# Causal attention on one core: another written order of all steps, eight slots for the exponentials in place of six

## The reference, cut to what matters

```python
x = L0_attn_x                               # (4, 2048, 256)
xn = _layernorm(x)
s = attention(xn)                           # 16 heads of 16, causal
g = silu(two_local_attention_layers(xn))    # 8 heads of 64, window 128, and a gated MLP
return x + s * g

# attention, for every batch row and head
scores = q @ k.T * scale                    # scale = 16 ** -0.5
scores = where(k_pos > q_pos, -inf, scores)
p = softmax(scores)                         # over k
out = p @ v
```

## Time and profile before

| what | value |
|---|---|
| median of 3 runs | 4990.12 us (4989.68 to 5007.07) |
| profiled execution | 4986.53 us, span 4984.7 us |
| TensorE (PE) busy | 4590.0 us, 92% |
| VectorE busy | 3673.8 us, 74% |
| ScalarE busy | 2994.0 us, 60% |
| GpSimd busy | 1342.6 us, 27% |
| mean granted TensorE clock | 0.949 |

### The profile page before, as it was taken

One profiled execution on the slowest core, in us unless ns is written; L12 is line 12 of the kernel. 1 busy time (PEld: TensorE's weight loads), 2 busy tenths in 40 slices (PEclk: granted clock), 3 DMA queues, 4 the chain that ended last, 5 costly groups with the idle time before them and its releaser, 6 DMA issues. The chain is left out here.

```text
span 4984.7 us, 91933 instructions
## 1 busy us (share of the span) xinstructions
PE 4590.0 (92%) x32224; PEld 3005.9 (60%) x32224; DVE 3673.8 (74%) x7585; ACT 2994.0 (60%) x6873; POOL 1342.6 (27%) x1844
## 2 busy tenths in 40 slices
PE   8589999999999996899999999995999999999986
PEld 7433334333334332577777777764677777777766
DVE  7488887887878883777777777754777777777746
ACT  3157776777777774456565666651665656566642
POOL 3112111121111121433333333311433333333300
PEclk9789998999999997899999999996999999999998
DMA  8722432222432222000000000001000000000008
GB/s 300 212 34 35 57 45 36 36 35 41 55 42 36 36 36 69 5 9 18 10 18 10 14 13 14 14 9 65 5 18 10 18 10 18 10 14 14 14 6 277
DMA packets 174917, 214.21 MB, mean 43 GB/s; under 512 B 75068, under 2 KB 126228, under 8 KB 168340
## 3 DMA queue, kind: packets, MB, share of 16 engines
q1 hardware_dynamic: 174484, 208.56, 18.4%
HBM read 124.05 MB, written 83.89 MB: 42 GB/s over the span
## 5 line engine op out<-in xcount | busy, mean ns | idle before, releaser
L601 ACT ACTIVATE a_pt<-a_ring 128x512 f32<-128x512 f32 (+3 forms) x2560 | 1182.8, 542 | 474.4 <-PE a_ring L712 458.8
L652 DVE TENSOR_REDUCE a_mx<-a_ring 128x2 f32<-128x1024 f32 (+3 forms) x1092 | 1129.6, 1064 | 267.9 <-PE a_ring L732 164.3
L996 POOL TENSOR_TENSOR l_rn<-l_ssm,l_half 128x8 f32<-128x8 f32 x256 | 431.7, 1687 | 941.0 <-DVE l_ssm L1278 941.0
L725 PE MATMUL a_ring<-a_ks,a_qs 48*128 48x512 f32 (+3 forms) x2560 | 568.3, 439 | 115.7 <-DMA a_v_in<-v_d 83.1
L712 PE MATMUL a_ring<-a_qs,a_ks 49*128 49x512 f32 (+3 forms) x2560 | 574.3, 456 | 50.8 <-ACT a_pt L601 26.9
L749 PE MATMUL a_ot<-a_pt,a_vt 128*32 128x512 f32 (+3 forms) x5120 | 613.0, 559 | 1.8 <-ACT a_os L607 1.3
L712 PEld LDWEIGHTS a_ring<-a_qs,a_ks 49*128 49x128 f32 x2560 | 255.1, 193 | 454.9 <-ACT a_pt L601 271.8
L1097 ACT ACTIVATE l_pr<-l_pr,l_negm 128x256 f32<-128x256 f32 (+1 forms) x1024 | 501.8, 495 | 6.5 <-DVE l_negm L1330 6.1
L725 PEld LDWEIGHTS a_ring<-a_ks,a_qs 48*128 48x128 f32 x2560 | 265.9, 196 | 380.4 <-ACT a_pt L601 175.7
L575 POOL TENSOR_TENSOR a_gate<-a_gate 128x1 f32<-128x1 f32 x512 | 99.6, 195 | 1413.6 <-ACT a_pt L601 1403.4
L1003 POOL TENSOR_TENSOR l_work<-l_work,l_rot 128x512 f32<-128x512 f32 x256 | 357.4, 1397 | 396.0 <-DVE l_work L1286 396.0
(11 more groups left out here) (173 smaller groups left out, 9070.4 us busy)
## 6 DMA issues: line engine op xcount, KB each, us to landing
qk_d<-p_parts SPq DMA_DIRECT2D x16, 2048.0 KB, 10.4
a_qs<-qk_d SPq DMA_DIRECT2D x96, 256.0 KB, 8.5
a_ks<-qk_d SPq DMA_DIRECT2D x96, 256.0 KB, 18.5
x_d<-l_dx SPq DMA_DIRECT2D x32, 512.0 KB, 2.8
l_xt<-x_d SPq DMA_DIRECT2D x24, 513.0 KB, 3.8
p_x_in<-x SPq DMA_DIRECT2D x16, 512.0 KB, 8.8
x_d<-p_xt SPq DMA_DIRECT2D x16, 512.0 KB, 5.1
v_d<-p_vt SPq DMA_DIRECT2D x16, 512.0 KB, 10.8
```

Source lines behind the costliest of these rows:

```text
L601: act.activation(pt[:, (g * STEPS + s) % NPT, 2 * piece + f, q0:CHUNK], bank("step", g, k, f)[:, q0:CHUNK], ACT.Exp).then_inc(exp_done.sem, 1)
L652: r = dve.tensor_reduce(mx[:, pr, :, t, kc], ring[:, banks[0]:banks[1] + 1, 0:w], AX.X, ALU.max)
L725: mm = pe.matmul(bank("unit", G, n, f)[:, 0:w], qs[rows, v, pr, q0:q0 + P], ks[rows, v, pr, kc * CHUNK:kc * CHUNK + w], start=True, stop=k ...
L996: pool.tensor_tensor(out=rn[:, a * HEADS:(a + 1) * HEADS], in0=ssm[:, a * HEADS:(a + 1) * HEADS], in1=half[:, 0:HEADS], op=ALU.pow).then_i ...
```

## The change

NPT, the number of slots for exponentials, goes from 6 to 8. All 208 entries of TensorE's order are written anew, and the places of the rarer entries on the other queues follow. The set of entries for a group is the same. The units run two less ahead of the steps (45 to 124 in place of 47 to 126). The distance between a step and the weighing of its slot changes from place to place. On SyncE, out 1 and row_out 4 change places. No function that computes is changed.

```diff
-        NPT = 6
+        NPT = 8
...
         def tensor_order(do):
-            do("step", 0); do("unit", 47); do("weigh", -4); do("step", 1); do("unit", 48); do("step", 2)
-            do("unit", 49); do("weigh", -3); do("step", 3); do("unit", 50); do("step", 4); do("step", 5)
-            do("weigh", -2); do("weigh", -1); do("step", 6); do("step", 7); do("unit", 51); do("unit", 52)
-            do("step", 8); do("unit", 53); do("weigh", 0); do("step", 9); do("unit", 54); do("weigh", 1)
-            do("step", 10); do("unit", 55); do("step", 11); do("unit", 56); do("weigh", 2); do("row_out", 2)
-            do("unit", 57); do("step", 12); do("step", 13); do("out", -1); do("unit", 58); do("weigh", 3)
...
-            do("unit", 71); do("step", 25); do("unit", 72); do("weigh", 10); do("weigh", 11); do("unit", 73)
-            do("step", 26); do("unit", 74); do("weigh", 12); do("step", 27); do("unit", 75); do("step", 28)
-            do("unit", 76); do("step", 29); do("unit", 77); do("step", 30); do("unit", 78); do("weigh", 13)
-            do("unit", 79); do("step", 31); do("step", 32); do("weigh", 14); do("unit", 80); do("unit", 81)
-            do("step", 33); do("unit", 82); do("row_out", 3); do("step", 34); do("unit", 83); do("step", 35)
-            do("step", 36); do("weigh", 15); do("unit", 84); do("unit", 85); do("step", 37); do("unit", 86)
...
-            do("step", 48); do("weigh", 19); do("step", 49); do("unit", 96); do("step", 50); do("unit", 97)
-            do("weigh", 20); do("step", 51); do("unit", 98); do("step", 52); do("weigh", 21); do("unit", 99)
...
-            do("step", 75); do("weigh", 34); do("unit", 125); do("step", 76); do("step", 77); do("weigh", 35)
-            do("step", 78); do("step", 79); do("unit", 126); do("row_out", 5)
+            do("step", 0); do("unit", 45); do("step", 1); do("weigh", -4); do("unit", 46); do("step", 2)
+            do("unit", 47); do("weigh", -3); do("step", 3); do("weigh", -2); do("step", 4); do("step", 5)
+            do("unit", 48); do("weigh", -1); do("step", 6); do("unit", 49); do("step", 7); do("unit", 50)
+            do("weigh", 0); do("unit", 51); do("step", 8); do("unit", 52); do("step", 9); do("unit", 53)
+            do("weigh", 1); do("step", 10); do("unit", 54); do("weigh", 2); do("step", 11); do("unit", 55)
+            do("step", 12); do("row_out", 2); do("unit", 56); do("step", 13); do("out", -1); do("weigh", 3)
...
+            do("step", 28); do("weigh", 12); do("unit", 76); do("step", 29); do("step", 30); do("weigh", 13)
+            do("unit", 77); do("step", 31); do("unit", 78); do("weigh", 14); do("step", 32); do("unit", 79)
+            do("weigh", 15); do("unit", 80); do("step", 33); do("unit", 81); do("step", 34); do("unit", 82)
+            do("row_out", 3); do("out", 1); do("step", 35); do("unit", 83); do("step", 36); do("weigh", 16)
...
+            do("step", 46); do("unit", 90); do("step", 47); do("unit", 91); do("weigh", 20); do("step", 48)
+            do("unit", 92); do("step", 49); do("unit", 93); do("step", 50); do("unit", 94); do("step", 51)
+            do("unit", 95); do("weigh", 21); do("step", 52); do("unit", 96); do("unit", 97); do("step", 53)
...
+            do("step", 75); do("weigh", 34); do("step", 76); do("unit", 123); do("step", 77); do("unit", 124)
+            do("weigh", 35); do("step", 78); do("step", 79); do("row_out", 5)
...
-                do("row_out", 4); do("out", 1); do("out", 2)
+                do("out", 1); do("row_out", 4); do("out", 2)
...
-                for n in range(1, 8):
+                for n in range(1, 7):
                     do("step", n)
                 do("raw_out", -1)
-                for n in range(8, 12):
+                for n in range(7, 13):
                     do("step", n)
-                do("row_copy", 2); do("step", 12); do("step", 13); do("raw_out", 0)
+                do("row_copy", 2); do("step", 13); do("raw_out", 0)
...
-                do("row_copy", 4)
-                for n in range(45, 54):
-                    do("step", n)
-                do("raw_out", 2)
-                for n in range(54, 80):
+                do("raw_out", 2); do("step", 56); do("step", 57); do("step", 58); do("row_copy", 4)
+                for n in range(59, 80):
                     do("step", n)
```

More of the change, by code:

```diff
@@ L450, in tensor_order @@
[L450 to L454, removed]
@@ new lines, in tensor_order @@
+            do("step", 14); do("unit", 57); do("unit", 58); do("weigh", 4); do("step", 15); do("unit", 59)
+            do("step", 16); do("unit", 60); do("step", 17); do("unit", 61); do("weigh", 5); do("unit", 62)
+            do("step", 18); do("unit", 63); do("unit", 64); do("step", 19); do("out", 0); do("step", 20)
+            do("weigh", 6); do("step", 21); do("unit", 65); do("step", 22); do("unit", 66); do("weigh", 7)
+            do("unit", 67); do("unit", 68); do("step", 23); do("unit", 69); do("weigh", 8); do("step", 24)
@@ new lines, in tensor_order @@
+            do("unit", 92); do("step", 49); do("unit", 93); do("step", 50); do("unit", 94); do("step", 51)
+            do("unit", 95); do("weigh", 21); do("step", 52); do("unit", 96); do("unit", 97); do("step", 53)
+            do("weigh", 22); do("step", 54); do("unit", 98); do("step", 55); do("unit", 99); do("weigh", 23)
+            do("step", 56); do("unit", 100); do("unit", 101); do("weigh", 24); do("step", 57); do("unit", 102)
+            do("unit", 103); do("step", 58); do("weigh", 25); do("row_out", 4); do("step", 59); do("unit", 104)
@@ new lines, in tensor_order @@
+            do("step", 60); do("unit", 105); do("weigh", 26); do("unit", 106); do("step", 61); do("unit", 107)
+            do("step", 62); do("unit", 108); do("weigh", 27); do("step", 63); do("unit", 109); do("unit", 110)
+            do("step", 64); do("weigh", 28); do("step", 65); do("unit", 111); do("unit", 112); do("weigh", 29)
+            do("step", 66); do("unit", 113); do("step", 67); do("unit", 114); do("out", 2); do("step", 68)
+            do("unit", 115); do("weigh", 30); do("step", 69); do("unit", 116); do("step", 70); do("unit", 117)
@@ L461, in attend @@
+            do("weigh", 31); do("unit", 118); do("step", 71); do("unit", 119); do("step", 72); do("unit", 120)
+            do("weigh", 32); do("step", 73); do("unit", 121); do("weigh", 33); do("step", 74); do("unit", 122)
+            do("step", 75); do("weigh", 34); do("step", 76); do("unit", 123); do("step", 77); do("unit", 124)
+            do("weigh", 35); do("step", 78); do("step", 79); do("row_out", 5)
         held = [None] * NB
@@ L677, in around @@
             def around(do):
-                for n in range(0, 7):
-                    do("unit", n)
-                do("out", -3)
-                for n in range(7, 27):
+                do("unit", 0); do("unit", 1); do("unit", 2); do("out", -3)
+                for n in range(3, 35):
                     do("unit", n)
                 do("out", -2)
-                for n in range(27, 58):
+                for n in range(35, 57):
                     do("unit", n)
                 do("out", -1)
-                for n in range(58, 67):
+                for n in range(57, 65):
                     do("unit", n)
                 do("out", 0)
-                for n in range(67, 80):
+                for n in range(65, 80):
                     do("unit", n)
```

21 lines of the change are left out of this document (8 added, 13 removed).

## The result

The changed kernel is slower: 5046.51 us (median of 4 runs, 5043.51 to 5062.55) against 4994.23 us for the kernel before in the same comparison; ratio 1.0116, 95% interval [1.0088, 1.0144]. The ratio was estimated together with its interval from the runs of the comparison; the quotient of the two medians is 1.0105, inside the interval. The forecast was 4976 us and "same"; the range ended at 5022. The slower rival, a clock that falls between weighings 20 and 21, was named and had a chance of 0.20. It is what happened, at a higher price than I gave it.

The account below looks back on a forecast made before the run. TensorE was the busiest engine, losing clock mid-period in the attention stage. 15 x (-0.6 - 0.1) = -11 us, say -11 to -15, took 4986.5 to 4974; the runs' median, 3.6 above, gave 4977; forecast 4976 us, range 4930 to 5022.

Parts of the forecast that it names:

- slower rival: Between weighings 20 and 21 the clock falls where nothing covers it: 5016 us, 5025 with weigh 0 waiting; chance 0.20.
- 1. Trigger of the load: Next group's q, k, v load, queued behind row_out 2, starts 1.5 us later; bounds +1.1 and +1.9.
- 2. Work ahead of the wait: Before unit 80: two more units and one weighing; TensorE 1.7 us later, load wait from 2.6 to about 2.1 us.
- 3. Less work behind it: From unit 80 to the next group: two fewer units, one fewer weighing; -2.1 us a period.
- item 5(b): Stretch without a weighing moves to steps 48 to 51, units 92 to 95: 1.6 us in half the groups, +0.8.
- Item 5(a): Behind the load: a shorter wait keeps full clock in six groups, say, instead of three of 14; -0.5 us on average.
- Item 5(c): Two groups with lasting low clock, 13 us over the mean together: half regained as fall and wait separate, -0.4 a period.
- 6. Weighing and slots: Weighing positions and two more slots for exponentials: priced at 0, from -1.0 to +0.6 us a period.
- 7. Order inside: Sequence of entries within a group, alike in both orders: 0, plus or minus 1.0 us a period.
- 8. and 9. Queue and ends: Sync queue swap of row_out 4 and out 1: 0. Prologue -2.4 us, last group +1.7 to +2.4: together 0.

Follow-up runs that it names:

- b_slots8: The kernel before with eight slots for exponentials in place of six, order unchanged: ratio 0.9994 to the kernel before.
- a_twice_at_62: The changed kernel with the score matmuls of steps 62 to 64 done twice: ratio 1.0125 to the kernel before.
- a_spread: The changed kernel with weigh 21 behind unit 93 and weigh 22 behind unit 96, nothing added: ratio 1.0024 to the kernel before.
- b_load_late: The kernel before with row_out 2 and row_copy 2 one step later, behind step 12: ratio 1.0042 to the kernel before.
- a_load_at_11: The changed kernel with row_out 2 and row_copy 2 one step earlier, behind step 11: ratio 1.0053 to the kernel before.

## Why the prediction was wrong, point by point

1. Trigger of the load: right in kind. Forecast +1.5 us, bounds to +1.9; measured +1.9 (+16.5 for +14.6). One step's delay in the old order costs 1.4 us a period.
2. Work ahead of the wait: TensorE was to be free at +43.8 and its last weighing there ended at +43.8 (425.73 plus 1.06 us, in a group from 383.0). The wait was to shrink to 2.1 us and grew to 3.41, because the load began and ended later: unit 80 at +47.2, not +45.9. Part of that is the group I had picked: its load took 29.8 us from the first transfer to unit 80, while the mean of the 14 groups is 30.3 us before and 30.4 after (unit 80 at +44.9 and +46.9).
3. Less work behind it: forecast -2.1 us. From unit 80 to the end at full clock the group of the earlier trace rows took 57.6 us, the group from 1140.8 us, whose unit 80 comes at +45.4, took 101.5 - 45.4 = 56.1: -1.5.
4. So items 1 and 3 sum to about +0.4 us and not to -0.6. The difference is 15 us over the stage, and alone it would have kept the time inside the forecast's range.
5. The step that failed is item 5(b). I saw that the run moves, named its place and that nothing covers it, and then priced it at 1.6 us in half of the groups, +0.8 a period. It struck ten of 14. The kernels without these falls run 104.2 us a period for 108.2 in their profiled executions, and 0.9% less by the timed runs (1.0116 to 1.0024 or 1.0026), which is 3.1 us a period; both include the smaller loss at the load that came with it. Within the changed kernel's own trace, the ten groups with such a fall took 107.6 to 113.3 us, 109.7 on average, and the three that fell only behind the load 105.0 to 105.9: 4.2 us in ten of 14 groups, again 3.0 a period. The price came from the stretch up to weigh 13 alone, and from one of the two groups with a long low phase: in the five others that fell there the stretch took 4.7 to 5.2 us, little more than the 4.8 at full clock. The low clock goes on behind the stretch: from weigh 20 to weigh 24 it cost 3.1 us in one group of the changed kernel, and more after that. In the kernel before, a short fall near +38 ran into the load's wait, which hid part of it: the two groups with that fall alone waited 0.95 and 0.35 us for the load and took 101.7 and 101.4 us, against a wait of 1.26 us and 100.6 us in the group that never fell.
   Item 5(a) had the wrong sign: with a longer wait, 13 groups in place of nine fell behind the load. Item 5(c), 0.4 us back because fall and wait are apart, did not come. The pieces overlap: +0.4 and 3.1 are 3.5 us, and the period grew by 3.0.
6. Weighing and slots: right, nothing (b_slots8; 39.8 us of waits for 39.6).
7. Order inside: right, nothing. At full clock with the early load both orders take the same time within 0.5 us.
8. and 9. Queue and ends: nothing seen. The prologue is 41.9 us for 44.0, as forecast. In the profiled executions the stage is 47 us longer, and the unchanged part behind it 15 us longer (3041 to 3056 us); of the 17 profiled executions the kernel before has the shortest such part and the changed kernel the longest, so a quarter of the difference between these two executions lies outside the changed stage. The control a_twice_at_62, with the same falls and a ratio of 1.0125 on its own comparison, says that the loss itself is no such accident.

The rule of the Trainium skill that I weighed ("TensorE: Matmul & The Clock Gate", A second HAM failure mode: psum-queue depth-cycling) spoke for the slower rival, and the trace of the changed kernel agrees: ten groups lose clock with no idle piece over about 0.4 us in the run. I gave the trace's agreement in the prediction and then a chance of only 0.20 to what followed from it.

Shown by experiment: with the late load, taking the falls of the run between weighings 20 and 21 away is worth about 0.9%, and two unlike edits do it, six more matmuls in the run or its weighings placed otherwise, while the same matmuls elsewhere do not. The load a microsecond or two later costs 0.2 to 0.6% (1.0024 left in a_spread, 1.0042 in b_load_late, 1.0116 to 1.0053 in a_load_at_11); the slots and the rest of the order cost nothing that shows. The two parts are not independent, since each edit also changed how many groups fall at the other place. Open: what exactly decides whether a run loses clock. A run of seven did not in the old order, one of eight ahead of weigh 20 with narrow steps did, and in four of 14 groups of the changed kernel no fall begins at the same run.

## What to carry to other kernels

Where TensorE is nearly the bound and other engines give its banks back one by one, as here, try spreading its heavy work (here the weighings) evenly: look for the longest stretch between two of them, and read the granted clock by window behind it, not only within it. When a transfer is late by a few microseconds in every round, look at what stands ahead of its issue in its queue: here two small transfers that could have gone 6.5 us earlier, worth 1.1%. A fall of the clock that ran into a wait looked cheap here, about 1 us in a group; the groups of the changed kernel with a fall where nothing was awaited took 2.1 to 7.8 us more than the 105.5 us, on average, of those that fell only behind the load.

## What the runs showed of the hardware that was not expected

More matmuls made the kernel faster: six more score matmuls a group, in the right place, took about 45 us off by the ratios (1.0116 to 1.0026), and the same six elsewhere took nothing off (1.0125).

TensorE's busy share doesn't show where it lacks work. In the 16 us from +60 it is busy 15.16 us in a group that loses clock (0.79) and 14.42 us in one of the cut run that keeps it (1.00), with 110 matmuls done in the first and 134 in the second: slow matmuls fill the time.
